# Linear attention's state as four products on TensorE's column quarters, written into the block diagonal by ScalarE

## The reference

```
kh = layernorm(ctx @ wk) * gamma + beta          # per context row, 128 channels
vh = layernorm(ctx @ wv) * gamma + beta
k' = (relu(kh) + 1e-6) * mask;  vh = vh * mask
kv[h] = sum over the 1500 rows of k'[h] (8) x vh[h] (8)     # the state, one 8 x 8 block per head
z[h]  = 1 / (q'[h] . sum k'[h] + 1e-6)
att[h] = q'[h] @ kv[h] * z[h]
```

## Time and profile before

| what | value |
|---|---|
| median of 3 runs | 807.87 us (803.96, 807.87, 809.74) |
| profiled execution | 808.45 us, its span 806.6 us |
| mean granted TensorE clock | 0.943 |
| busy over the whole span | PE 692.5, PEld 479.7, DVE 536.2, ACT 511.1, POOL 270.0 us |
| chain that ended last | PE 60%, DVE 20%, issue 9%, ACT 7%, POOL 2% |
| L524, context product | 384 passes, 92.8 us busy |
| L538, state product | 384 passes, 56.7 us busy |
| L1067 and L1070, gamma and beta | 48 each, 61.1 and 64.4 us busy |
| L876, values | 192, 54.8 us busy, mean 368 ns |

### The profile page before, as it was taken

One profiled execution on the slowest core, in us unless ns is written; L12 is line 12 of the kernel. 1 busy time (PEld: TensorE's weight loads), 2 busy tenths in 40 slices (PEclk: granted clock), 3 DMA queues, 4 the chain that ended last, 5 costly groups with the idle time before them and its releaser, 6 DMA issues.

```text
span 806.6 us, 19439 instructions
## 1 busy us (share of the span) xinstructions
PE 692.5 (86%) x7276; PEld 479.7 (59%) x7283; DVE 536.2 (66%) x1251; ACT 511.1 (63%) x806; POOL 270.0 (33%) x322
## 2 busy tenths in 40 slices
PE   3698999977457998898898899889889999799997
PEld 3477777765223556566565556555656666467776
DVE  5799999987657876786786777778767672311111
ACT  4477777772243876776776786686778768343531
POOL 3388888880333023213304314222231110000000
PEclk9899999996555999999999999999999999699999
DMA  4122222334607065367256346536635661110110
GB/s 134 38 77 80 91 97 76 122 103 29 132 2 169 14 151 128 75 124 156 72 112 150 95 106 125 127 75 126 161 82 122 125 136 44 46 43 28 53 39 24
DMA packets 59377, 74.40 MB, mean 92 GB/s; under 512 B 35320, under 2 KB 40178, under 8 KB 59306
## 3 DMA queue, kind: packets, MB, share of 16 engines
q1 hardware_dynamic: 59306, 73.39, 38.3%
HBM read 32.35 MB, written 1.40 MB: 42 GB/s over the span
## 4 chain that ended last, share of the span: by engine, by line
PE 60%; DVE 20%; issue 9%; ACT 7%; POOL 2%; DVEq 1%; ACTq 0%; POOLq 0%; another core or an unknown queue 0%
PE ps L727 10%; PE ps L635 8%; DVE mx L1540 7%; PE ps L786 6%; PE ps L798 6%; PE ps L627 5%; PE ps L714 5%; PE ps L621 4%; PE ps L524 4%; PE ps L538 3%; DVE ss L1244 2%; PE ps L655 2%; ACT arena L863 2%; DVE arena L1264 2%; ACT P L975 1%
## 5 line engine op out<-in xcount | busy, mean ns | idle before, releaser
L975 ACT ACTIVATE P<-ps,kbias,kscale 125x896 f32<-125x896 f32 x192 | 210.6, 1098 | 98.3 <-PE ps L714 95.1
L1540 DVE TENSOR_REDUCE mx<-ps 128x1 f32<-128x500 f32 x336 | 216.0, 673 | 77.4 <-PE ps L635 72.8
L635 PE MATMUL ps<-KP,Qb 128*128 128x500 bf16 x336 | 132.3, 395 | 5.2 <-POOL Qb L1102 2.6
L727 PE MATMUL ps<-P,Vp 125*32 125x112 f32 x3072 | 113.4, 265 | 1.6 <-ACT P L975 1.1
L727 PEld LDWEIGHTS ps<-P,Vp 125*32 125x32 f32 x3072 | 67.1, 109 | 51.5 <-issue 29.5
L1083 POOL TENSOR_TENSOR KP<-kvall,KP 128x1500 bf16<-128x1500 f32 x16 | 48.5, 3031 | 140.5 <-ACT KP L919 140.5
L524 PE MATMUL ps<-wkv,cT 128*125 128x256 f32 x384 | 92.8, 385 | 0.5 <-ACT arena L876 0.5
L524 PEld LDWEIGHTS ps<-wkv,cT 128*125 128x125 f32 x384 | 70.0, 192 | 9.9 <-issue 0.9
L627 PE MATMUL ps<-wv_sb,cT 128*125 128x128 f32 x384 | 56.8, 294 | 18.6 <-DVE silu L1447 7.1
L714 PE MATMUL ps<-QS,KS 128*128 128x112 bf16 x768 | 69.9, 214 | 3.3 <-issue 1.9
L876 ACT ACTIVATE arena<-ps,arena 125x128 f32<-125x128 f32 x192 | 54.8, 368 | 27.5 <-DVE arena L1258 13.9
(11 more groups left out here) (212 smaller groups left out, 1021.0 us busy)
## 6 DMA issues: line engine op xcount, KB each, us to landing
cT<-ctxT_dram SPq DMA_DIRECT2D x32, 750.0 KB, 4.2
KS<-KP SPq DMA_DIRECT2D x48, 375.0 KB, 7.1
arena<-KP SPq DMA_DIRECT2D x48, 375.0 KB, 7.5
QS<-QD SPq DMA_DIRECT2D x96, 28.0 KB, 5.6
wgu<-w_dram SPq DMA_DIRECT2D x8, 256.0 KB, 3.1
silu<-w_dram SPq DMA_DIRECT2D x8, 256.0 KB, 3.0
x<-xh_dram SPq DMA_DIRECT2D x1, 512.0 KB, 3.5
mixed<-att SPq DMA_DIRECT2D x16, 28.0 KB
```

The lines of the kernel that those rows point to most:

```text
L635: ins = nc.tensor.matmul(ps[:, bank, 0:KCW], q[:, 128 * c:128 * c + 128], KP[par][0][:, KCW * k:KCW * k + KCW], start=True, stop=True)
L727: ins = nc.tensor.matmul(ps[r:r + PW, 7, c:c + PAIRW], Vp[par][0:TK, t, p, :], P[t % 2][0:TK, PAIRW * p:PAIRW * p + PAIRW], start=(t == 0 ...
L975: nc.scalar.activation(P[t % 2][0:TK, :].rearrange("p (k n) -> p k n", k=2), src, ACT.Exp, scale=kscale[0:TK, bass.ds(n, 1)], bias=kbias[0 ...
L1540: ins = v.tensor_reduce(mx[:, c, k:k + 1], ps[:, bank, 0:KCW], AX.X, ALU.max)
```

## The change

The state product is split: instead of 128 key columns by 130, each tile makes four products of 32 key columns by 34 (32 value columns and the two extra ones), one for each quarter of the columns, each into its own 32 partitions of the same PSUM bank and the same 34 columns. So the bank holds the four diagonal blocks of 32 by 32 under one another. For this the extra columns stand four times in `VN`, behind each quarter of the values, which GpSimd's small product writes. VectorE's `state` works on 32 columns with masks of 32, writes a small tile `kvc`, and ScalarE's new `expand` copies its four quarters to their places in `kvall`, which GpSimd sets to zero at the start. The columns of `kvall` are ordered by quarter (32 values, 4 key sums), and `normalise` reads them so. TensorE waits for `kv_put` instead of `kv_read` before the product with the queries.

```
             for t in range(GT):
-                ins = nc.tensor.matmul(ps[:, 6 + par, 0:D + 2], KN[0:TK, s6, t, :], VN[0:TK, s6, t, 0:D + 2],
-                                       start=(g == 0 and t == 0), stop=(g == NG - 1 and t == GT - 1))
+                for j in range(NQ):
+                    r = QUAD * j
+                    ins = nc.tensor.matmul(ps[r:r + QUAD, 6 + par, 0:QUAD + 2], KN[0:TK, s6, t, r:r + QUAD],
+                                           VN[0:TK, s6, t, j, 0:QUAD + 2], start=(g == 0 and t == 0),
+                                           stop=(g == NG - 1 and t == GT - 1), skip_group_check=True)
...
-            pe.wait_ge(sem("kv_read"), B)
+            pe.wait_ge(sem("kv_put"), B)
...
-                    ins = nc.scalar.activation(VN[0:TK, k, t, 0:D], ps2[0:TK, c0:c0 + D], ACT.Copy,
-                                               scale=VN[0:TK, k, t, D + 2:D + 3])
+                    ins = nc.scalar.activation(VN[0:TK, k, t, :, 0:QUAD],
+                                               ps2[0:TK, c0:c0 + D].rearrange("p (j d) -> p j d", j=NQ), ACT.Copy,
+                                               scale=VN[0:TK, k, t, 0, QUAD + 2:QUAD + 3])
...
+            def expand(b, par):
+                act.wait_ge(sem("kv_read"), b + 1)
+                for j in range(NQ):
+                    r = QUAD * j
+                    ins = nc.scalar.copy(kvall[r:r + QUAD, bass.ds(b, 1), BLK * j:BLK * j + BLK],
+                                         kvc[r:r + QUAD, par, :].unsqueeze(1))
+                ins.then_inc(sem("kv_put"), 1)
...
                         deviation(n, k)
+                        if g == 1 and not first:
+                            expand(2 * i + par - 2, par)
+            act.wait_ge(sem("kv_zeroed"), 1)
             in_pairs(act, pair, B // 2)
             values(NG * B - 1, SLOTS - 1)
+            expand(B - 2, 0)
+            expand(B - 1, 1)
...
+            nc.gpsimd.memset(kvall[:], 0.0).then_inc(sem("kv_zeroed"), 1)
...
-                nc.gpsimd.tensor_tensor(VN[0:TK, k, :, D:D + 3], emcat[0:TK, bass.ds(b * T + GT * g, GT), :],
-                                        rk[0:TK, k % 2, :, 1:4], ALU.mult).then_inc(sem("emc_ready"), 1)
+                nc.gpsimd.tensor_tensor(VN[0:TK, k, :, :, QUAD:VB],
+                                        bc(emcat[0:TK, bass.ds(b * T + GT * g, GT), :], 2, [TK, GT, NQ, 3]),
+                                        bc(rk[0:TK, k % 2, :, 1:4], 2, [TK, GT, NQ, 3]),
+                                        ALU.mult).then_inc(sem("emc_ready"), 1)
...
+            v.tensor_reduce(gquad[:], gmask[:].rearrange("p (j d) -> p d j", j=NQ), AX.X, ALU.add)
+            v.tensor_reduce(bquad[:], bmask[:].rearrange("p (j d) -> p d j", j=NQ), AX.X, ALU.add)
+            step(v.tensor_reduce(hquad[:], hmask[:].rearrange("p (j h) -> p h j", j=NQ), AX.X, ALU.add))
...
+                if not first_pair:
+                    dve.wait_ge(sem("kv_put"), b - 1)
                 kv = ps[:, 6 + par, :]
-                v.tensor_tensor(kvtmp[:, par, :], kv[:, 0:D], gmask[:], ALU.mult).then_inc(sem("kvt_ready"), 1)
-                v.tensor_tensor(kvall[:, bass.ds(b, 1), D:KVW], hmask[:].unsqueeze(1),
-                                bc(kv[:, D + 1:D + 2], 1, [128, 1, H]), ALU.mult)
+                v.tensor_tensor(kvtmp[:, par, :], kv[:, 0:QUAD], gquad[:], ALU.mult).then_inc(sem("kvt_ready"), 1)
+                v.tensor_tensor(kvc[:, par, QUAD:BLK], hquad[:], kv[:, QUAD + 1:QUAD + 2].broadcast_to([128, HQD]), ALU.mult)
                 dve.wait_ge(sem("kvt_ready"), b + 1)
-                v.scalar_tensor_tensor(kvall[:, bass.ds(b, 1), 0:D], bmask[:].unsqueeze(1), kv[:, D:D + 1],
-                                       kvtmp[:, par, :].unsqueeze(1), ALU.mult, ALU.add).then_inc(sem("kv_read"), 1)
+                v.scalar_tensor_tensor(kvc[:, par, 0:QUAD], bquad[:], kv[:, QUAD:QUAD + 1],
+                                       kvtmp[:, par, :], ALU.mult, ALU.add).then_inc(sem("kv_read"), 1)
```

More of the change, by code:

```diff
@@ L34 @@
 KVW = D + H
+QUAD = 32
+NQ = D // QUAD
+HQD = H // NQ
+BLK = QUAD + HQD
+VB = QUAD + 3
 EPS_LN, EPS_IN = 1e-5, 1e-6
@@ L255, in build @@
         kvall = sb("kvall", [128, B, KVW])
-        kvtmp = sb("kvtmp", [128, 2, D])
+        kvtmp = sb("kvtmp", [128, 2, QUAD])
+        kvc = sb("kvc", [128, 2, BLK])
+        gquad = sb("gquad", [128, QUAD])
+        bquad = sb("bquad", [128, QUAD])
+        hquad = sb("hquad", [128, HQD])
         ss = sb("ss", [128, 2, 2 * GT])
@@ L259, in build @@
         rk = sb("rk", [128, 2, GT, 4])
-        arena = sb("arena", [128, 8264])
+        arena = sb("arena", [128, 8480])
         KN = arena[:, 0:3072].rearrange("p (s t d) -> p s t d", s=6, t=GT)
-        VN = arena[:, 3072:6216].rearrange("p (s t d) -> p s t d", s=6, t=GT)
-        SQ = arena[:, 6216:8264].rearrange("p (s n) -> p s n", s=2)
+        VN = arena[:, 3072:6432].rearrange("p (s t j d) -> p s t j d", s=6, t=GT, j=NQ)
+        SQ = arena[:, 6432:8480].rearrange("p (s n) -> p s n", s=2)
         hT = arena[:, 0:2 * FC * B * S].rearrange("p (s c n) -> p s c n", s=2, c=FC)
@@ L1230, in _ @@
             hm3 = bc(hmask[:], 2, [128, H, DK])
-            v.tensor_tensor(gmask[:].rearrange("p (h d) -> p h d", h=H),
-                            row[:, GAMMA, :].rearrange("p (h d) -> p h d", h=H), hm3, ALU.mult)
+            step(v.tensor_tensor(gmask[:].rearrange("p (h d) -> p h d", h=H),
+                                 row[:, GAMMA, :].rearrange("p (h d) -> p h d", h=H), hm3, ALU.mult))
             step(v.tensor_tensor(bmask[:].rearrange("p (h d) -> p h d", h=H),
                                  row[:, BETA, :].rearrange("p (h d) -> p h d", h=H), hm3, ALU.mult))
+            v.tensor_reduce(gquad[:], gmask[:].rearrange("p (j d) -> p d j", j=NQ), AX.X, ALU.add)
+            v.tensor_reduce(bquad[:], bmask[:].rearrange("p (j d) -> p d j", j=NQ), AX.X, ALU.add)
+            step(v.tensor_reduce(hquad[:], hmask[:].rearrange("p (j h) -> p h j", j=NQ), AX.X, ALU.add))
             dve.wait_ge(sem("q0_ps"), 1)
@@ L1264, in relu, with state @@
                 v.tensor_scalar(kn, kn, 0.0, EPS_IN, ALU.max, ALU.add).then_inc(sem("kp_ready"), 1)
-            def state(b, par):
+            def state(b, par, first_pair=False):
                 dve.wait_ge(sem("kv_done"), NG * (b + 1) + SLOTS)
+                if not first_pair:
+                    dve.wait_ge(sem("kv_put"), b - 1)
                 kv = ps[:, 6 + par, :]
-                v.tensor_tensor(kvtmp[:, par, :], kv[:, 0:D], gmask[:], ALU.mult).then_inc(sem("kvt_ready"), 1)
-                v.tensor_tensor(kvall[:, bass.ds(b, 1), D:KVW], hmask[:].unsqueeze(1),
-                                bc(kv[:, D + 1:D + 2], 1, [128, 1, H]), ALU.mult)
+                v.tensor_tensor(kvtmp[:, par, :], kv[:, 0:QUAD], gquad[:], ALU.mult).then_inc(sem("kvt_ready"), 1)
+                v.tensor_tensor(kvc[:, par, QUAD:BLK], hquad[:], kv[:, QUAD + 1:QUAD + 2].broadcast_to([128, HQD]), ALU.mult)
                 dve.wait_ge(sem("kvt_ready"), b + 1)
-                v.scalar_tensor_tensor(kvall[:, bass.ds(b, 1), 0:D], bmask[:].unsqueeze(1), kv[:, D:D + 1],
-                                       kvtmp[:, par, :].unsqueeze(1), ALU.mult, ALU.add).then_inc(sem("kv_read"), 1)
+                v.scalar_tensor_tensor(kvc[:, par, 0:QUAD], bquad[:], kv[:, QUAD:QUAD + 1],
+                                       kvtmp[:, par, :], ALU.mult, ALU.add).then_inc(sem("kv_read"), 1)
             def pair(i):
-                first = isinstance(i, int) and i == 0
+                first, second = (isinstance(i, int) and i == k for k in range(2))
                 for par in range(2):
@@ L1286, in pair @@
                         if g == 0 and not first:
-                            state(b - 2, par)
+                            state(b - 2, par, second)
                         keys(b, n, k, first)
-            in_pairs(dve, pair, B // 2)
+            pair(0)
+            pair(1)
+            with dve.Fori(2, B // 2) as i:
+                pair(i)
             last = NG * B - 1
@@ L1299, in nd @@
                 bank, c = nd_place(t)
-                return ps[:, bank, c:c + KVW]
+                return ps[:, bank, c:c + KVW].rearrange("p (j n) -> p j n", j=NQ)
             def normalise(tiles):
                 for t in tiles:
-                    ins = v.tensor_scalar(xn[:, t, 0:H], nd(t)[:, D:KVW], EPS_IN, None, ALU.add)
+                    ins = v.tensor_scalar(xn[:, t, 0:H].rearrange("p (j h) -> p j h", j=NQ), nd(t)[:, :, QUAD:BLK],
+                                          EPS_IN, None, ALU.add)
                 step(ins)
@@ L1308, in normalise @@
                 for t in tiles:
-                    ins = v.tensor_tensor(att[:, t, :].rearrange("p (h d) -> p h d", h=H),
-                                          nd(t)[:, 0:D].rearrange("p (h d) -> p h d", h=H),
-                                          bc(xn[:, t, H:2 * H], 2, [128, H, DK]), ALU.mult)
```

(4 more changed lines are left out.)

## The result

The changed kernel took 821.2 us (median of 4 runs, 820.75 to 822.85) against 807.05 for the kernel before (4 runs, 803.96 to 809.74): ratio 1.0188, 95% interval 1.0153 to 1.0222. It is slower. The profiled execution took 821.05 with a span of 819.2, 12.6 above the span of before; the mean granted clock was 0.935 (0.943 before). The medians differ by 14.15: the profiled execution of before was 1.4 above its median, that of the change at its own. So the two traces have 12.6 to explain.

A forecast was written before the change was run, and what follows sets the result against it. GpSimd's loop, with VectorE instructions standing until GpSimd's running one ends, was taken to bound the kernel. State -1.5, small product +2.3 and end -0.75 summed to +0.05 us: 807.9 as median, range 802 to 825.

The forecast's parts named there:

- the slower rival: ScalarE's four copies exceed 0.72 us, so the third group's relu stands behind GpSimd's beta: +15 us, 823; chance 0.25.
- The two slow rivals: Copies too long for their slack on ScalarE (823, chance 0.25); TensorE's clock falling in the loop (836, chance 0.04).
- The bound: Linear attention loop: GpSimd's work sets the 9.43 us batch, with VectorE instructions standing until GpSimd's running one is over.
- Column quarters: TensorE's state product: 32 load and pass pairs take 0.4 us, 0.74 with tile shape changes, against 1.16; zero effect on time.
- State on 32 columns: VectorE's last state operation still waits for beta but ends 0.11 us sooner behind it: -1.5 us over 14 batches.
- Small product: GpSimd writes 48 elements for 12: +0.076 us per group, two groups per batch exposed, +2.3 us over 15 batches.
- ScalarE's expand: Four copies between the second group's deviation and third group's square take 0.5 us, at worst 0.77; no cost below 0.72.
- The cover: Delay the third group's VectorE relu can take without loss while it stands for GpSimd's gamma: 0.64, or 0.72 us.
- The rival's sum: Third relu behind beta opens a second GpSimd hole, 1.07 us per batch, 14 batches: +15 us, 823; chance 0.25.
- The start: Before the loop: three more VectorE reduces, about 0.3 us each, and GpSimd's 4.9 us memset fall into existing waits.
- The end: Behind the loop, uncovered: last product -1.15, last state step twice -0.1, last expand +0.6; together -0.75 us.
- The rival with half the batches at the lower level: TensorE's clock falls to 1.2 GHz in the loop, some 13 us per batch instead of 9.4: +28, 836; chance 0.04.

The follow-up runs named there:

- the PSUM run: Kernel before, with the gamma product of VectorE's last state operation written to free PSUM columns instead of SBUF tile kvtmp: 800.96 us, ratio 0.9915.
- The run on the same partitions: Kernel before plus four idle ScalarE copies per batch, all on partitions 0 to 31, 18 columns each: 808.78 us, period 9.42.
- The quarters alone: Changed kernel with expand moved out of the loop, copying 14 batches at once and then the last two: 807.13 us, ratio 1.0004.
- the four copies alone: Kernel before plus four idle ScalarE copies of 32 partitions by 36 per batch, result read by nobody: 819.37 us, ratio 1.0164.

## Where the prediction was right and where it was wrong, point by point

The forecast of no change (807.9, 0.63 for "same") failed, and the slower rival, to which it gave 0.25, happened as described. 821.2 lies inside the range of 802 to 825 only because the range was drawn out to hold that rival. That it comes within 2 us of the rival's 823 is partly luck: terms that the rival's sum left out cancel in part (below). The two slow rivals have 0.25 and 0.04, which makes 0.29 and not the 0.27 that the summary of the chances gives.

- **The bound.** Right: GpSimd's loop, with VectorE's instructions that stand behind GpSimd's running one. The third relu and L1308 ended just behind one in the loop, and taking work off TensorE changed nothing (98.20 us busy for 116.85 with the copies behind the loop, and the same period).
- **Column quarters.** Estimated 0.4 for 32 pairs and no gain; 0.46 measured, and ratio 1.0004 with the copies out of the loop. Right. The charge of 0.17 behind the product was too high: the next context product starts at 107.88, before its modelled end at 107.95, and its weight loads begin 0.04 behind the last ones of the quarters; no pause for the change of tile shape shows there.
- **State on 32 columns.** Right: L1308 still ended just behind beta (110.04 + 1.03 = 111.07, beta 111.02), 0.05 behind for 0.15, where 0.04 was taken; hole -0.10 per batch, -1.4 in all. That the width doesn't decide, the narrow L1308 shows (median 1043 ns); that the second SBUF input does, the PSUM run. The Trainium skill, SBUF — State Buffer, Who interferes with whom, says the same, and 353 ns for 941 agrees. The relu, which the prediction counted among the rows that agree with that rule, has only one input in SBUF and stands all the same, while the reduce, also with one, doesn't (1.22 us beside gamma, 104.94 to 106.16); no run here isolates what makes the relu stand.
- **Small product.** Estimated 0.28 us, measured 0.27. On GpSimd's way it costs 0.05 to 0.06 per group (104.31 to 104.54 is 0.23, for 0.17 before), where 0.076 was taken; and since the new hole hides a second one, it is paid once per batch and not twice.
- **ScalarE's expand: the step that failed.** "So a copy takes the queue 0.08 + 0.03 = 0.11 and four take 0.44", with 0.77 as the upper end. Measured: 0.23 and 0.92, above both. The cover of 0.64 to 0.72 was right (three copies, 0.69, fit), so the mechanism was right and this one term was mis-sized. Both rows it came from the earlier trace rows are of instructions on the same partitions, which overlap; the four copies go to 0, 32, 64 and 96 and don't. The Trainium skill, ScalarE: Activation LUTs, What ACT_TABLE_LOAD costs, has back-to-back ACTIVATEs overlap by about 93 ns. The run on the same partitions agrees (0.199 long, 0.10 apart); on different ones the measurement differs from it, and decides. Address arithmetic was the wrong suspicion: the copies behind the loop, with fixed addresses, are 0.23 apart too (8 in 1.84 us), and those on the same partitions are 0.10 apart with moving addresses.
- **The rival's sum.** 1.07 per batch for the second hole; 1.06 measured. Its 15 us left out the narrower L1308 and shorter betas (-0.22 per batch together), the wider small product (+0.05), the clock (+1.2) and the end (-0.6); 12.5 came of 14 batches at 0.89.
- **The start.** Right: nothing was lost. The memset took 2.07 us for an estimate of 4.9, the three reduces 0.38, 0.37 and 0.18, and the first L1308 came 0.66 earlier than L1274 had; in the other runs of this document that start lies between 47.4 and 48.6, so the 0.66 isn't the change's gain.
- **The end.** Estimated -0.75, measured -0.60 from the last relu's start to the output product (2.75 for 3.35). Product -1.39 (estimate -1.15), state -0.25 (-0.2), expand +1.03 (+0.6), again the copies.
- **The clock.** The rival with half the batches at the lower level (0.04) didn't happen. In three short stretches (67.08 to 70.49, 87.56 to 90.97, 108.04 to 111.45) the granted clock was 0.50, 1.2 GHz; the eight passes at 107.88 took 3.66 us for 1.96, and the three together cost 1.2 us. The quarters alone (clock 1.00 in the window, TensorE busy 98.20 us of 128.87) and the four copies alone (1.00, 105.07) had no such fall; the change has both, with 94.01. Both together are not enough for it: with the copies ahead of the values (1.00, 97.95) it didn't fall either. Why it falls in the change was not isolated.

## What to carry to other kernels

Before putting small work into a queue, work out the slack at that place and take the price from a row with the same pattern of partitions: here two copies cost nothing, three 0.17 us per batch and four 0.96. The four copies of the change were free two steps earlier in the queue. And where an instruction's shortest execution is a third of its median, ask for what it stands: moving one operand to PSUM gave 0.85%, which narrowing the same instruction to a quarter didn't.

## What the runs showed of the hardware

- ScalarE's plain copies of 32 partitions: 0.10 us apart on the same partitions, 0.23 apart when each goes to another 32 (0.20 and 0.22 us long). This holds with and without a store address that moves with the batch (163.60 to 164.02 for four on the same partitions with fixed addresses).
- VectorE's `scalar_tensor_tensor` with two SBUF inputs, behind a GpSimd operation: ends 0.05 behind it with 32 columns, 0.15 with 128; with one of the two in PSUM it takes 252 and 353 ns and doesn't wait.
- The stand goes both ways: where the relu started 0.01 us before beta, beta took 1.54 us instead of 1.33.
- TensorE: 32 pairs of 32 weight columns and 34 moving columns took 0.46 us at 2.4 GHz and 0.68 at 1.2 GHz; the 8 passes of 130 columns that they replace took 1.16 and 2.12.
